# Cross-attention with a mixture-of-experts block: two shared weights split during the last projections, a group's last addition in halves, the x transposes one slot on

## The reference

```python
x = x + xattn(layernorm(x), context)     # context: 257 image rows and 1344 text rows a batch
x = x + moe(layernorm(x))
# xattn: q = rms(x Wq + b), k, v and k_img, v_img from the two parts of the context, 16 heads of 32;
#        out = (softmax(q k) v + softmax(q k_img) v_img) Wo + b
# moe:   32 experts with routing, and a shared expert for every row:
shared = silu(x @ shared_gate.T) * (x @ shared_up.T) @ shared_down.T
```

## Time and profile before

| | |
|---|---|
| median of 3 runs | 1189.96 us (1187.46 to 1190.88) |
| the profiled execution | 1194.59 us, span 1192.8 us |
| PE busy | 1116.2 us, 94% of the span |
| DVE busy | 856.9 us, 72% |
| ACT busy | 650.6 us, 55% |
| attention and projections | 0 to 823 us of the span |
| expert part | 829 us to the end |

### The profile page before, as it was taken

The page is one execution under the profiler, slowest core; times in us unless marked ns, Lnnn a source line. Parts: engine busy times, 40 slices in busy tenths (PEclk is TensorE's granted clock), DMA queues, the critical chain, the costliest instruction groups (busy, mean ns, idle before and its releaser), DMA issues. The chain is left out here.

```text
span 1192.8 us, 21823 instructions
## 1 busy us (share of the span) xinstructions
PE 1116.2 (94%) x8948; PEld 415.7 (35%) x8948; DVE 856.9 (72%) x1056; ACT 650.6 (55%) x916; POOL 202.1 (17%) x307
## 2 busy tenths in 40 slices
PE   7899999999999989999999999887999989999996
PEld 3342223344222334322233432222544433333332
DVE  6777889897898988788889879997789842222221
ACT  5559997444999644699955469883311121221121
POOL 1220000243000024300002430002100021333442
PEclk9999999999999999999999999999999999999999
DMA  8851000768200096900028780104813337999742
GB/s 299 199 109 43 2 2 10 194 135 201 54 2 2 20 228 136 203 8 2 2 72 194 171 215 31 36 3 136 359 60 109 113 113 285 348 317 313 215 62 33
DMA packets 142860, 150.15 MB, mean 126 GB/s; under 512 B 108833, under 2 KB 109089, under 8 KB 137761
## 3 DMA queue, kind: packets, MB, share of 16 engines
q1 hardware_dynamic: 135328, 131.57, 38.1%
q0 software_dynamic: 5120, 10.82, 4.9%
q10 hardware_dynamic: 2304, 6.29, 2.2%
HBM read 101.96 MB, written 21.51 MB: 104 GB/s over the span
## 5 line engine op out<-in xcount | busy, mean ns | idle before, releaser
L718 ACT ACTIVATE work<-ps 128x1024 f32<-128x1024 f32 x384 | 372.3, 1022 | 30.7 <-PE ps L1215 15.0
L1221 PE MATMUL ps<-work,vals 128*32 128x512 f32 (+2 forms) x1664 | 220.3, 600 | 3.8 <-DVE nums L963 2.1
L1072 PE MATMUL ps<-wts,work 128*128 128x512 f16 x864 | 194.9, 379 | 11.1 <-DVE work L777 10.7
L1215 PE MATMUL ps<-quer,keys 32*128 32x512 f16 x2496 | 171.9, 377 | 22.2 <-ACT work L718 14.9
L975 DVE TENSOR_TENSOR work<-work 128x2048 f32<-128x2048 f32 x64 | 146.6, 2291 | 6.2 <-ACT work L718 0.5
L975 DVE TENSOR_TENSOR attn<-attn,work 128x2048 f32<-128x2048 f32 x62 | 142.0, 2290 | 5.4 <-ACT work L718 0.5
L1072 PEld LDWEIGHTS ps<-wts,work 128*128 128x128 f16 x864 | 83.3, 98 | 118.7 <-issue 19.3
L2040 PE MATMUL ps<-wring,xgt 128*80 128x512 f32 x256 | 114.9, 592 | 0.0
L1866 DVE COPY xgt<-ps 128x320 f32<-128x320 f32 x32 | 15.7, 491 | 137.8 <-PE ps L2031 137.8
L1072 PE MATMUL ps<-wts,hl 128*128 128x512 f16 x432 | 101.1, 386 | 12.0 <-DVE wts L759 7.3
L533 POOL TENSOR_SCALAR small<-small 128x1 f32<-128x1 f32 x68 | 20.5, 301 | 534.9 <-ACT work L628 534.9
(11 more groups left out here) (221 smaller groups left out, 1402.5 us busy)
## 6 DMA issues: line engine op xcount, KB each, us to landing
wring<-in_wx SPq DMA_DIRECT2D x32, 1536.0 KB, 9.1
raw<-in_ctx SPq DMA_DIRECT2D x52, 256.0 KB, 3.3
rb<-sums_inverse ACTq DMA_DIRECT2D x48, 128.0 KB, 3.8
work<-in_x SPq DMA_DIRECT2D x8, 512.0 KB, 4.8
table<-nums SPq DMA_DIRECT2D x16, 256.0 KB, 2.5
work<-in_x SPq DMA_DIRECT2D x12, 256.0 KB, 3.5
x<-work SPq DMA_DIRECT2D x12, 256.0 KB, 2.6
x2t_rows<-nums SPq DMA_DIRECT2D x12, 256.0 KB, 2.5
```

Source lines behind the costliest of these rows:

```text
L718: act.activation(prob[0:rows, s % PROBS, 2 * half:2 * half + 2, :], ps[0:rows, 2 * pair:2 * pair + 2, :], ACT.Exp, scale=SCALE, bias=pad i ...
L1072: mm = pe.matmul(out, lhs(a, c)[:, cols], wts[:, w, z, c * D:(c + 1) * D], start=(k == 0), stop=(k == len(steps) - 1))
L1215: mm = pe.matmul(ps[:, 2 * pair + h % 2, :], k[h * HD:(h + 1) * HD, :], q[h * HD:(h + 1) * HD, :], start=(e == 0), stop=(e == len(terms) - 1))
L1221: return pe.matmul(ps[h * HD:(h + 1) * HD, NUM, :], vals[a:z, ORDER[n], g * P + h * HD:g * P + (h + 1) * HD], prob[a:z, s % PROBS, h, :], ...
```

## The change

Four things:

1. `ffn_weight` of SG and SU moves from the attention of the last batch into its projections, slots 10 and 14 of DVE's list. Their loads move with it, into SP's slots 8 and 12, and use a staging tile at 172 KB that the weighing has left free by then. SD stays in the attention, in group 1.
2. The last of the nine text additions of a group becomes two of 128x1024: one ahead of the copy of the numerators, one behind it.
3. All work on x moves one slot on, on DVE, POOL, ACT and SP alike. PE's waits stay where they are.
4. The two multiplications 128x512 of `weigh` become one of 128x1024.

```diff
 # SP
+                        if b == B - 1 and i == 8:
+                            sp.wait_ge(a_at, gn(q, NG - 1))
+                            sp.dma_start(sstage[SG][:, :], d["w3"][SG]).then_inc(s_fw[SG], 16)
+                        if b == B - 1 and i == 12:
+                            sp.wait_ge(f_wlo, 3 * (bb // B) + 1)
+                            sp.dma_start(sstage[SU][:, :], d["w3"][SU]).then_inc(s_fw[SU], 16)
...
-                        if i in (5, 7, 9, 11):
-                            turn_x(bb, (i - 5) // 2)
+                        if i in (6, 8, 10, 12):
+                            turn_x(bb, (i - 6) // 2)
...
-                for i in range(3):
-                    sp.dma_start(sstage[i][:, :], d["w3"][i]).then_inc(s_fw[i], 16)
+                sp.dma_start(sstage[SD][:, :], d["w3"][SD]).then_inc(s_fw[SD], 16)
 # POOL
-                        if i in (3, 5, 7, 9):
-                            x_scale(bb, (i - 3) // 2)
+                        if i in (4, 6, 8, 10):
+                            x_scale(bb, (i - 4) // 2)
 # ACT
-                    if i in (4, 6, 8, 10):
-                        x_high(bb, (i - 4) // 2)
+                    if i in (5, 7, 9, 11):
+                        x_high(bb, (i - 5) // 2)
 # DVE
-                image = own(dve.tensor_tensor(nums[:, g, 1, :], nums[:, g, 1, :], rb[:, g % 2, 1, :], ALU.mult))
-                dve.tensor_tensor(nums[:, g, 0, :], nums[:, g, 0, :], rb[:, g % 2, 0, :], ALU.mult).then_inc(a_mt, 1)
-                dve.wait_ge(d_link, image)
+                both = nums[:, g, :, :].rearrange("p t q -> p (t q)")
+                dve.tensor_tensor(both, both, rb[:, g % 2, :, :].rearrange("p t q -> p (t q)"), ALU.mult).then_inc(a_mt, 1)
...
-                    if i in (3, 5, 7, 9):
-                        x_stats(bb, (i - 3) // 2)
                     if i in (4, 6, 8, 10):
-                        x_normed(bb, (i - 4) // 2)
+                        x_stats(bb, (i - 4) // 2)
                     if i in (5, 7, 9, 11):
-                        x_low(bb, (i - 5) // 2)
+                        x_normed(bb, (i - 5) // 2)
+                    if i in (6, 8, 10, 12):
+                        x_low(bb, (i - 6) // 2)
...
+                    if b == B - 1 and i in (10, 14):
+                        ffn_weight(p, (i - 10) // 4)
...
-                    if bb == B - 1 and g > 0:
-                        ffn_weight(p, g - 1)
+                    if b == B - 1 and g == 1:
+                        ffn_weight(p, SD)
...
                         if n == KT - 1:
+                            parted = not (b == B - 1 and g == NG - 1)
+                            if parted:
+                                dve.wait_ge(a_sum, added(bb, g, n - 5))
+                                dve.tensor_tensor(acc[:, 0:2 * L], acc[:, 0:2 * L], cur[:, 0:2 * L], ALU.add)
                             dve.wait_ge(a_av, step(bb, s))
                             dve.tensor_copy(nums[:, g, 0, :], ps[:, NUM, :]).then_inc(a_nt, 1)
+                            if parted:
+                                dve.tensor_tensor(acc[:, 2 * L:], acc[:, 2 * L:], cur[:, 2 * L:], ALU.add).then_inc(a_sum, 1)
+                                continue
```

More of the change, by code:

```diff
@@ L120, in __init__ @@
         self.swt = [self.sg, self.su, self.sd]
-        self.sstage = [at("sgs", 0, [P, NC * D], F32), at("sus", 8 * KB_, [P, NC * D], F32),
+        self.sstage = [at("sgs", 172 * KB_, [P, NC * D], F32), at("sus", 172 * KB_, [P, NC * D], F32),
                        at("sds", 16 * KB_, [P, NC * D], F32)]
@@ L867, in ffn_weight @@
             def ffn_weight(p, i):
+                if i == SG:
+                    dve.wait_ge(k_mm, slot((p + 1) * B - 1, 2))
+                    dve.wait_ge(v_mm, kvn((p + 1) * B - 1, 2))
                 dve.wait_ge(s_fw[i], 16 * (2 * p + 2 if i == 0 else p + 1))
@@ L947, in sums_and_results @@
                         image_sum(bb, g)
-                    elif b == B - 1 and g > 0:
-                        ffn_weight(p, g - 1)
                     if b > 0 and g < 2:
```

## The result

The changed kernel takes 1231.12 us, the median of 5 runs (1230.94 to 1233.44), beside 1190.88 us for the kernel before (5 runs, 1187.46 to 1192.05): a ratio of 1.0345 with a 95% interval of 1.0328 to 1.0362. It is slower, as forecast, but by 40.2 us instead of 23.5, above the upper end of the range.

A forecast was written before the change was run, and what follows sets the result against it. PE bounds the projections, waiting for DVE's low halves; in the attention PE, ACT and DVE run nearly in step. 5.0 + 8.0 + 8.0 - 2.0 - 0.5 + 5.0 = +23.5 on 1189.96 gives 1213.5 us, range 1199 to 1225.

The forecast's parts named there:

- The third x transpose late at slot 12: Projections, slot 12: issued behind slot 9's key transpose, it lands 3.6 us late, with DVE's 0.9 us together 4.5.
- the lower bound: Third x transpose's delay, batches 1 and 2: 3.0 us, since DVE's bias of slot 9 could begin some 1.5 us earlier.
- The first x tile eats the gain: Projections, slot 8: PE, ready about 1.7 us sooner, stands 2.5 us for the first x transpose; the gain is gone.
- Batch 0: First batch's projections: third x tile 4.6 us later, second tile late too; +5.0 us, bounds 3.7 and 6.5.
- Batches 1 and 2: Projections of these batches: 4.0 us lost in each by the x work, within 3.0 to 6.4; together +8.0.
- The last batch: Its projections: +8.0 us, 4.0 from the x work and 4 from the weight splits moved in (bounds 0 and 6).
- It misses slot 14 by 2 us or more: Last batch's projections: the fourth x transpose, behind the 1 MB load, lands at 692.7 or later, slot 14 due at 690.6.
- The last attention: Last batch's attention: two of three weight splits go, 3.2 us less about 1.2 for a later copy; -2.0, within -3.5 and -1.
- The halves and the weighing: Attention: -0.05 us at each of 12 boundaries by halved additions, a start saved by the merged multiplication; together -0.5.
- The rival that the copy binds: Attention: PE waits for the numerators' copy at each of 12 boundaries, 0.4 us instead of -0.05; 1218.9 us, 10%.
- The clock: PE's granted clock halves after long stands in the projections: three falls of 1.7 us, +5.0, between none and nine (15).
- the clock falls at every stand: Rival, projections: all nine PE stands are followed by a fall to half clock; 1223.8 us, 12%.

The follow-up runs named there:

- sp_only: The kernel before with only SP's x transposes one slot on, x work on DVE, POOL and ACT on old slots: 1216.26 us (before 1190.34).
- no_halves: The changed kernel with the last addition of a group whole again, the other three parts kept: 1226.31 us (before 1190.34).
- x_mid: The changed kernel with the x transpose issued right behind the key transpose, ahead of the store and residual load: 1222.54 us (before 1190.34).
- warm2: The changed kernel with extra matmuls, results overwritten, filling PE's stands in all batches but batch 0: 1222.05 us (before 1190.62).
- load_late: The changed kernel with x transposes ahead of key transposes in SP's list and SU's load behind the last x transpose: 1201.12 us (before 1190.34).
- x_back: The changed kernel with the x work of DVE, POOL, ACT and SP back on its old slots: 1197.12 us (before 1189.15).

## Why the prediction was wrong

Its sign and its mechanism were right. Point by point, against the profile:

- *The third x transpose late at slot 12.* Right in place and cause; the stand of 4.5 us measured 5.28, 4.85 and 4.29 in batches 1 to 3. The key transpose goes out 6.03 us after slot 10's start, where it was 5.83 (671.15 less 665.32 in the last batch of before), but DVE's 0.9 us ahead of the key are in it: with DVE's list as before (sp_only) it is 5.08. So DVE lost 0.75 us of its lag, half of the 1.5 that the lower bound allowed for, while PE stood at slot 8. The landing was 4.7, 4.2 and 3.7 us instead of 3.2; I had that in the bound, not in the sum.
- *The first x tile eats the gain.* Right: stands of 2.81, 2.46 and 2.43 us, forecast 2.5. Counted from the last score before, PE was ready for slot 8 2.6, 1.9 and 0.6 us sooner, forecast 1.7.
- *Batch 0.* +6.0, of it 1.7 by the clock, so 4.3 for a forecast of 5.0, which is inside the scatter of that stage. But the places were others: PE's timeline has 2.0 us each at slots 8 and 10 (the first two rows; the profile names no releaser for the first, but the x transpose issued at 51.96 lands 3.3 us later, at 55.3), and only 0.77 at slot 12 (the last).

```profile
55.32 9.62 PE L1086 MATMUL ps<-wts,work 128*128 128x512 f16 x36 [2.03 <-issue]
66.94 5.34 PE L1086 MATMUL ps<-wts,work 128*128 128x512 f16 x24 [2.00 <-DMA work<-work]
...
75.64 2.75 PE L1086 MATMUL ps<-wts,work 128*128 128x512 f16 x12 [0.77 <-DVE work L801]
```

- *Batches 1 and 2.* 8.5 and 8.4 less 3.4 each by the clock: 5.1 and 5.0 for 4.0.
- *The last batch.* 18.9 less 6.8: 12.1 for 8.0. "It misses slot 14 by 2 us or more" was priced at its lower end, and the stand there was 4.11: behind the load of 1 MB the key transpose lands in 8.3 us, and the next transpose holds SP until the load is in.
- *The last attention.* -1.6 for -2.0, with some luck: two splits away bring 2.6 (109.2 us in no_halves), and the halves beside the remaining one take 1.0 back, but in x_mid, warm2 and load_late a fall of the clock left only -0.2 to -0.3.
- *The halves and the weighing.* +0.5 for -0.5 in the first three batches. The rival that the copy binds was half right: PE does wait for it, 6.8 us in all instead of 2.1 (part 5 of the profile page, the numerators), but at the nine plain boundaries the scores get only 0.4 us longer by it.

```profile
L1235 PE MATMUL ps<-work,vals 128*32 128x512 f32 (+2 forms) x1664 | 220.3, 600 | 9.9 <-DVE nums L974 6.8
```

- *The clock.* "I take three falls, +5.0, between none and nine" is **the step that failed**. The trace shows 15 us of it, three times as much, and filling the stands of three batches gave 9 to 13 back. I had counted nine stands, and nine of 2.0 us or more there are, with a lower clock behind eight. The price of 1.7 us a fall was right; their number was not. This one choice is 10 of the 17 us that I missed by the stages; the last batch is 4, batches 1 and 2 are 2.1, and the attention 1.4, less 0.7 in the first batch; these last three are about as large as the scatter of one profile. The rival "the clock falls at every stand" (1223.8 us, given 12%) was the right case; the last batch and the smaller sizes above put the time 7 us over even that.

The rule that I set beside the row spoke for it: the Trainium skill ("TensorE: Matmul & The Clock Gate", Part 1) says that the default is the throttled state and that activity releases it. The trace agrees for eight of nine stands; it does not for the one of 2.00 us in batch 0, nor for the stand of 3.21 us in sp_only, behind which the clock stayed at 1.00. I had set the one fall of the earlier trace rows against waits that left the clock alone, but none of those was over 1.2 us; for stands of 2.5 and 3.6 us the only row was the one with the fall. The rule as I shortened it does not say how long a stand has to be; only rows could tell that.

## What to carry to other kernels

Before moving a transfer one step on, look at what stands ahead of it in the issuing engine's list, not only at its own inputs: the same x work one slot on cost 34 us, and 30 of the 40 us came back by one row of SP's list. Where PE will stand as long as here (2 to 5 us), price a fall of the clock at each stand, 1.7 us here, and put "no fall" into the bounds, not into the sum. A small cost beside a lagging engine isn't small: the half addition cost 0.4 us at nine boundaries together and 4.5 us beside two weight splits.

## What was not expected of the hardware

- Whether the clock falls isn't fixed by a stand's length at these lengths: it fell behind stands of 2.03, 2.43 and 2.46 us in the changed kernel, not behind 2.00 there nor behind 3.21 in sp_only. Behind the same stand of 2.36 us it fell in five profiles and not in three. One kernel's executions differ with it: those of the halves by 8.5 us, at mean granted clocks of 0.995 and 0.988.
- The load of SU landed in 5.3 us in the profile of one kernel (no_halves) and in 8.6 in another's (the changed kernel) from the same place of the list; the stand at slot 14 was 1.14 and 4.11 us accordingly.
- A DMA transpose can hold SP itself: the issue that takes 1.24 us took 4.63 behind that load, and 3.80 in x_back; both times SP was free within 0.03 us of the load's landing. In no_halves it took 2.58, until 0.5 us behind the landing.
